# Dense experts of a graph network: logits and last bias on VectorE, tables made a stage earlier, one group finished ahead, inverse roots by Newton steps

## The reference, cut to what matters

```
feat = mean(x, axis=0)                      # one batch: feat = x
w = softmax(feat @ Wr + br)                 # 6250 x 8 shares
h = relu(bn(x @ W1[e] + b1, g1, be1, m1, v1))   # each expert e, 256 -> 256
h = relu(bn(h @ W2[e] + b2, g2, be2, m2, v2))
y = h @ Wo[e] + bo[e]
out = sum over e of w[:, e] * y[e]          # added to x
```

## Time and profile before

| | |
|---|---|
| median of 3 runs (lowest, highest) | 4462.22 us (4454.69, 4463.83) |
| profiled execution, its own time | 4459.09 us |
| its span, first to last instruction | 4457.3 us |
| mean granted TensorE clock over the span | 0.814 |
| TensorE matmul, weight load | 3334.8 us (75%), 2512.1 us (56%) |
| VectorE | 2672.3 us (60%) |
| ScalarE | 1572.2 us (35%) |
| GpSimd | 2067.7 us (46%) |
| dense stage, first to last instruction | about 3331 to 4457 us |
| second rows stage | about 1916 to 2091 us |

### The profile page before, as it was taken

One profiled execution on the slowest core, in us unless ns is written; L12 is line 12 of the kernel. 1 busy time (PEld: TensorE's weight loads), 2 busy tenths in 40 slices (PEclk: granted clock), 3 DMA queues, 4 the chain that ended last, 5 costly groups with the idle time before them and its releaser, 6 DMA issues. The chain is left out here.

```text
span 4457.3 us, 72937 instructions
## 1 busy us (share of the span) xinstructions
PE 3334.8 (75%) x16240; PEld 2512.1 (56%) x16240; DVE 2672.3 (60%) x8449; ACT 1572.2 (35%) x4383; POOL 2067.7 (46%) x2095
## 2 busy tenths in 40 slices
PE   5276667776666789964566666666659999999999
PEld 3144444444444578843344444444438888888888
DVE  8488999999987866654565565656555322222221
ACT  2233343334332224431333333333323434333343
POOL 0477777777770034365777777777730000000000
PEclk9677787777876579966677777777779999999999
DMA  4344444444454147644444444444461000000000
GB/s 123 81 106 107 107 108 107 107 107 107 107 99 87 37 126 193 171 114 99 107 106 106 106 106 106 105 106 105 105 80 35 5 7 5 7 5 7 5 7 8
DMA packets 386919, 369.85 MB, mean 83 GB/s; under 512 B 253644, under 2 KB 313708, under 8 KB 386562
## 3 DMA queue, kind: packets, MB, share of 16 engines
q0 software_dynamic: 107072, 272.84, 24.9%
q1 hardware_dynamic: 277094, 92.40, 9.4%
q10 hardware_dynamic: 2396, 0.84, 0.1%
HBM read 324.13 MB, written 41.59 MB: 82 GB/s over the span
## 5 line engine op out<-in xcount | busy, mean ns | idle before, releaser
L694 POOL DMA_INDIRECT g_G<-rows,g_pack x1856 | 1806.8, 973 | 756.1 <-issue 480.0
L727 PE MATMUL bank<-g_G,g_MB 128*125 128x260 f32 x1856 | 654.7, 499 | 207.1 <-DVE acc L933 205.9
L933 DVE SCALAR_TENSOR_TENSOR acc<-acc,g_c,bank 125x65 f32 (+1 forms) x2320 | 618.2, 315 | 147.5 <-PE bank L727 73.1
L1375 DVE SCALAR_TENSOR_TENSOR X<-bank,e_cw,X 125x256 f32 (+1 forms) x400 | 175.2, 479 | 795.6 <-PE bank L1201 795.6
L727 PE MATMUL bank<-g_G,g_M 128*125 128x257 f32 x1856 | 633.6, 489 | 20.7 <-DVE acc L933 20.6
L727 PEld LDWEIGHTS bank<-g_G,g_MB 128*125 128x125 f32 x1856 | 418.4, 243 | 348.9 <-DVE acc L933 242.4
L1271 ACT ACTIVATE e_h<-bank,e_bi_c,e_sc_c 128x250 f32<-128x250 f32 x800 | 403.6, 555 | 560.3 <-PE bank L1192 422.3
L798 ACT ACTIVATE g_mt_d<-bank,unode 125x256 bf16<-125x256 f32 x928 | 383.3, 463 | 457.7 <-PE bank L712 457.2
L727 PEld LDWEIGHTS bank<-g_G,g_M 128*125 128x125 f32 x1856 | 418.3, 241 | 147.4 <-DVE acc L933 26.5
L1201 PE MATMUL bank<-e_w,e_h 128*125 128x256 f32 x1600 | 379.3, 380 | 3.1 <-ACT e_h L1271 3.1
L1192 PE MATMUL bank<-e_h,e_w 128*128 128x250 f32 x1600 | 377.6, 378 | 1.2 <-ACT e_h L1271 1.2
(11 more groups left out here) (299 smaller groups left out, 4141.3 us busy)
## 6 DMA issues: line engine op xcount, KB each, us to landing
g_G<-rows,g_pack POOLq DMA_INDIRECT x1856
acc<-in_edge_attr SPq DMA_DIRECT2D x50, 476.0 KB
g_pack<-edge_pack SPq DMA_DIRECT2D x928, 2.0 KB
g_drow<-edge_dst SPq DMA_DIRECT2D x928, 1.0 KB
expert_out<-x_y SPq DMA_DIRECT2D x54, 256.0 KB
g_qe<-edge_q SPq DMA_DIRECT2D x464, 1.0 KB
rows<-acc SPq DMA_DIRECT2D x25, 227.5 KB
rows<-n_T SPq DMA_DIRECT2D x25, 224.9 KB
```

The costliest lines, as they stand in the source:

```text
L694: nc.gpsimd.indirect_dma_start(G[:, r, q, :], None, rows_d[l], bass.IndirectOffsetOnAxis(ap=pack[:, r, q, 0:1], axis=0)).then_inc(S(p + f" ...
L727: mm_ = nc.tensor.matmul(sum_bank(r, k, u)[0:TN, 0:HW], left, G[:, rk, q, :], start=(c == 0), stop=(c == C - 1))
L933: ins = nc.vector.scalar_tensor_tensor(at, at, c1[:, rk, u, h:h + 1], sum_bank(r, k, u)[0:TN, h * W:(h + 1) * W], ALU.mult, ALU.add)
L1375: ins = nc.vector.scalar_tensor_tensor(xt, bank[4 + u][0:TN, 0:D], cw[:, r, u, e:e + 1], xt, ALU.mult, ALU.add)
```

## The change

- Router: `rows(1)` turns the router matrix and stores it to DRAM (`router_d`); the dense stage loads it to all partitions (`wrb`, 1 MB). Each logit is a multiply with sum on VectorE (`dot`: 16 per group, four in each of the slots 1 to 4), `shares` moves to slot 5, `weigh` to slot 5, `normal_shares` to slot 6, `normal` to slot 1, `turn` to slot 4. `logits`, `turn_shares` and `turned_shares` go.
- Last bias: `bo` is loaded to all partitions (1 MB); `add_bias` runs on VectorE for each expert, in every slot, behind the collect of the expert before. `last_bias` on TensorE goes.
- Tables of the batch norm, and the weights of expert 0, are loaded in `rows(1)`, the tables turned and finished there. They lie in SBUF through `attention(1)`.
- One group is finished ahead, with a root on ScalarE; group 1 is finished in slot 1 of group 0, and groups 2 to 24 in slots 3 to 6 of groups 0 to 5. Their inverse roots come from a bit trick and three Newton steps on VectorE (`root`, 12 operations on up to 8 columns). The first 6 groups (`STATIC`) are written out instead of 4.

```diff
 # rows(1): loads on SyncE ahead of its loop
+ for q, nm in enumerate(names):
+     sp.dma_start(etab_r[q * NX:(q + 1) * NX, :], a[nm]).then_inc(S("etab_in"), 16)
+ sp.dma_start(ewr[:, :, :], a["L1_ffn_Wr"]...).then_inc(S("etab_in"), 16)
+ sp.dma_start(br[:, :], ...).then_inc(S("ebr_in"), 16)
+ for k, nm in enumerate(("L1_ffn_W1", "L1_ffn_W2", "L1_ffn_Wo")):
+     sp.dma_start(wa[k], a[nm][0, :, :]...).then_inc(S("ewa_in"), 16)
 ...
   run(sp, slot)
+ sp.wait_ge(S("ewrT"), 1)
+ sp.dma_start(router_d, ewrT[:, :]).then_inc(S("router_out"), 16)
+ sp.wait_ge(S("router_out"), 16)
 # rows(1), i == 3: TensorE turns the tables and the router, ScalarE copies them out and takes 2 roots;
 # VectorE behind its loop: 10 operations to scale and shift
 # dense_experts, SyncE
- for e in range(NX): ... 3 weights each
+ for c in CUTS:
+     sp.dma_start(wrb[c, :, :], router_d.unsqueeze(0).broadcast_to([TN, NX, D])[c])...
+ load(1)
+ for c in CUTS:
+     sp.dma_start(bo[c, :, :], a["L1_ffn_bo"].unsqueeze(0).broadcast_to([TN, NX, D])[c])...
+ for e in range(2, NX):
+     load(e)
 # ScalarE, slot
  relu(1, ...); relu(0, i, i * NX + e, e)
+ if isinstance(i, int) and i == 0 and e == 1:
+     weigh(0)
  if follows(i):
-     if e == 2: turned(i + 1, 1 - r)
-     if e == 4: weigh(i + 1)
-     if e == 5: turned_shares(i + 1)
+     if e == 4: turned(i + 1, 1 - r)
+     if e == 5: weigh(i + 1)
 # VectorE
+ def dot(g, r, e):
+     if e == 0:
+         v.wait_ge(S(p + "xn"), g + 1)
+         held(v, p + "xn_seen")
+     for u in range(GT):
+         n_ = e * GT + u
+         if n_ >= 2:
+             v.wait_ge(S(p + "dot"), g * NX * GT + (n_ - 1))
+         nc.vector.tensor_tensor_reduce(junk[:, n_ % 2, :], xn[:, u, :], wrb[:, e, :], 1.0, 0.0, ALU.mult, ALU.add,
+                                        dots[:, r, u, e:e + 1]).then_inc(S(p + "dot"), 1)
+ def add_bias(i, r, e):
+     if e:
+         v.wait_ge(S(p + "o"), i * NX + e)
+     else:
+         v.wait_ge(S(p + "xn"), i + 1)
+         v.wait_ge(S(p + "cw"), i + 1)
+     held(v, p + "o_seen")
+     for u in range(GT):
+         xt = xtile(i * GT + u)
+         ins = nc.vector.scalar_tensor_tensor(xt, bo[:, e, :], cw[:, r, u, e:e + 1], xt, ALU.mult, ALU.add)
+     ins.then_inc(S(p + "biased"), 1)
  def slot(i, r, t):
      for e in range(NX):
+         if follows(i) and e == 6: normal_shares(i + 1, 1 - r)
          collect(...)
+         add_bias(i, r, e)
          if follows(i):
+             if e == 1:
+                 if isinstance(i, int) and i == 0:
+                     finish(1)
+                     root(1, FIRST)
+                 normal(i + 1)
+             if 1 <= e <= 4:
+                 dot(i + 1, 1 - r, 2 * e - 2)
+                 dot(i + 1, 1 - r, 2 * e - 1)
+             if e == 5: shares(i + 1, 1 - r)
+             if early and e >= 3 and lo + e - 3 < hi:
+                 finish(lo + e - 3)
+     if early:
+         root(lo, hi)
+ invert(0, GT)
+ finish(0)
  ...
  normal(0)
+ invert(GT, NT)
+ v.wait_ge(S(p + "wrb_in"), ND)
+ for e in range(NX):
+     dot(0, 0, e)
  shares(0, 0)
  normal_shares(0, 0)
+ v.wait_ge(S(p + "bo_in"), ND)
```

More of the change, by code:

```diff
@@ L155, in xtile, with rows @@
             return X[:, bass.ds(t, 1), :].rearrange("p o d -> p (o d)")
-        def rows(l, acc, pos_i, share, sc):
+        def rows(l, acc, pos_i, share, pre, sc):
             H = HEADS[l]
@@ L364, in slot @@
                             mm.then_inc(S(p + "xT"), 1)
+                        if l == 1 and isinstance(i, int) and i == 3:
+                            pe.wait_ge(S("etab_in"), 16 * (NQ + 1))
+                            for k in range(2):
+                                nc.tensor.transpose(bank[2][:, k * P:k * P + NQ * NX], etab_r[:, k * P:(k + 1) * P], ident[0:NQ * NX, 0:NQ * NX])
+                            for k in range(2):
+                                mm = nc.tensor.transpose(bank[3][0:NX, k * P:(k + 1) * P], ewr[:, k, :], ident[:, :])
+                            mm.then_inc(S("etab_mm"), 1)
                     run(pe, slot)
@@ L1088, in dense_experts @@
             p = "e_"
[L1089 to L1099, removed]
+            FIRST, STATIC, EACH = 2, 6, 4
+            sc_c, bi_c, br, wa = pre
+            w1, w2, w3 = (sb(p + f"w{k}", [P, NX - 1, 2, D], F32, sc) for k in range(3))
+            bo = sb(p + "bo", [TN, NX, D], F32, sc)
+            wrb = sb(p + "wrb", [TN, NX, D], F32, sc)
+            junk = sb(p + "junk", [TN, 2, D], F32, sc)
+            dots = sb(p + "dots", [TN, 2, GT, NX], F32, sc)
             den = sb(p + "den", [TN, NT], F32, sc)
@@ L1142, in _ @@
                 def _(pe):
[L1143 to L1146, removed]
                     def turn(g, r):
@@ L1915, in build @@
             acc = sb("acc0", [TN, NT * HEADS[0] * (D // HEADS[0] + 1)], F32, s0)
-            for part in (lambda s2: rows(0, acc, None, None, s2), lambda s2: attention(0, acc, s2)):
+            for part in (lambda s2: rows(0, acc, None, None, None, s2), lambda s2: attention(0, acc, s2)):
                 with ExitStack() as s2:
@@ L1934, in build @@
                 with ExitStack() as s2:
-                    rows(1, acc, pos_i, share, s2)
+                    rows(1, acc, pos_i, share, pre, s2)
                 end_stage()
             acc1 = acc[:, 0:NT * (D + 1)]
-            for part in (lambda s2: attention(1, acc1, s2), lambda s2: dense_experts(acc1, s2)):
+            for part in (lambda s2: attention(1, acc1, s2), lambda s2: dense_experts(acc1, pre, s2)):
                 with ExitStack() as s2:
```

201 lines of the change are left out of this document (90 added, 111 removed).

## The result

The changed kernel takes 4415.02 us (median of 4; 4410.27 to 4416.63) against 4463.02 for the kernel before in the same session: ratio 0.9885, 95% interval [0.9864, 0.9906]. The forecast was 4431 in a range of 4402 to 4465, so the sign and the range held, and the gain, 48.0 us, is half as large again as the 31.6 forecast. One profiled execution of an experiment (four groups ahead) was a disturbed one at a mean clock of 0.716; its trace isn't compared.

The account below looks back on a forecast made before the run. TensorE was taken to bound the dense stage (busy 200 of 200 us). Start -9.5, groups 1 to 5 +5.9, border -3.5, groups 6 to 23 -25.2, rows stage +0.7 sum to -31.6: 4431 us, range 4402 to 4465.

Parts of the forecast that it names:

- rows stage and up to the first dense instruction: Second rows stage, paced by GpSimd's gathers: ends on the late store of the router rows, +0.7 us (0 to 1.9).
- layer 1: Start of the dense stage: one group instead of four finished before the root, so the first layer starts 16.9 us earlier.
- given back in group 0: Group 0: late first collect, overfull VectorE slot 1, late shares and lower clock, less removed TensorE work: +7.4 us.
- groups 1 to 5: Five written-out groups that also finish four groups each: VectorE late at the shares, TensorE waits; +5.9 us together.
- border: Between groups 2 and 3: ScalarE's wait for all variances and its table reload go, -3.5 us.
- eighteen groups: Groups 6 to 23: TensorE's removed 2.27 us less a new wait of 0.86, 1.4 gained each, -25.2 us.
- the steady wait: Looped groups: bias ahead of shares delays exponential and the relu queued behind it; TensorE loses 0.86 us (0.72 to 1.0).
- C: Rival, 15%: the exponential's lateness does not reach TensorE; steady groups gain the full 2.27 us, total 4409.
- An early group: ... +1.2: Each early static group: -2.27 us of TensorE work, +2.7 wait at the shares, +0.75 for the clock.
- A: Rival, 15%: summing halves the dot's rate, pitch 0.69 us; loop still fits, six early groups cost 2 us each, total 4444.
- B: Rival, 12%: VectorE becomes the bound in slots 1 to 4, from a dot pitch of 0.75 us; at 0.85, total 4523.
- D: Rival, 8%: the clock falls at each looped group's wait of 0.86 us, +27 us, total 4458, no change.

Follow-up runs that it names:

- four groups ahead: Against the changed kernel, four groups instead of one are finished ahead of the first root, none in slot 1 of group 0: 4412.79 us, ratio 0.9893.
- three dots: Against the changed kernel, every dot is done three times, the extra two into a tile that nobody reads: 4579.13 us, ratio 1.0267.
- two dots: Against the changed kernel, every dot is done twice, the second into a tile that nobody reads: 4443.66 us, ratio 0.9964.

## Why the prediction was right, and where its sizes were off

From the spans, term by term (us, forecast and measured): rows stage and up to the first dense instruction +0.7, +0.3; layer 1 -16.9, -17.0; given back in group 0 +7.4, +4.9; groups 1 to 5 +5.9, -2.7; border -3.5, -4.0; eighteen groups -25.2, -30.2. Sum -31.6, -48.7 (by unrounded terms). The misses don't cancel: 8.6 us of the 17.1 by which the sum is off lie in groups 1 to 5, 5.0 in the looped groups, 2.5 in group 0. The first term is not resolved: from the rows stage's first gather to the attention's first it is 182.1 us against 181.1 before, and 177.7 to 182.1 in the other runs with the same rows stage. It is not longer by more than 2, the sign of being wrong that the prediction named. The rows stage and the border had no run of their own.

*Right in mechanism and size:* what TensorE loses a group (2.27 forecast; 43.63 - 41.29 = 2.34 by the run with the later exponential), the start, and the border, whose 47.59 became an ordinary group.

*Right in mechanism, the steady wait too large:* 0.86 forecast, 0.66 measured, so groups of 41.95 instead of the 42.2 named (and of C's 41.4). The gap ahead of the bias, taken as 0.40, is 0.14 (collect to bias 1.02, of which 0.88 is collect's), so the exponential is 1.02 late and not 1.28. The result lies nearer to rival C's 4409 than to the forecast's 4431, but C is not what happens: the lateness does reach TensorE, and two runs got 18.7 and 23.3 us by removing it.

*The step that failed is "An early group: ... +1.2" in "First six groups".* Groups 1 to 5 gain 0.6 each instead (less 0.36 once, at the entry into the loop), and the wait above 2 us, named as a sign of being right, was 0.72 in group 0 and 1.47 to 1.82 in the others. VectorE's lateness at the shares was put at 2.0; 1.07 was measured (static less looped group). The slots 3 and 4 were put at 6.37 and take 5.85 and 5.86 (group 4's collects at 3537.39, 3543.24 and 3549.10). The dot accounts for it: its pitch is 0.345, below the forecast's lower bound of 0.40, and not 0.48, so four dots are 0.54 less; the smaller gap ahead of the bias and a gap of 0.17 ahead of the next collect make up for each other. And the half of 1.5 us of clock put on each such wait didn't come: after waits of 1.47 to 1.82 the layer took 1.99.

*Group 0:* the wait in slot 1 was 3.81 (5.1 forecast), slot 1 on VectorE 9.16 (3352.04 to 3361.20) instead of 10.1 by the same dots and smaller gaps. The wait at the shares was 0.72 (2.7 forecast). What is lost behind the wait, 1.77, came in slot 1 and not at the shares, where 1.5 had been put.

*Rivals.* A: no dot of 0.69; a pitch of 0.69, made on purpose, left the loop unchanged and cost most static groups 4.5 to 5.1 each (A's 2 us counted from a pitch of 0.48 and without the clock). B: shown at three dots, absent at one. D: the granted clock from 3600 to 3800 us, in the loop, is 1.00.

On the bias the rows answer the question left open: with both wide sources in SBUF (L1390) 481 ns, with one in PSUM (L1400) 479. The rule of the Trainium skill that a scalar-tensor-tensor operation with two 32-bit SBUF sources runs at half rate ("Vector Engine (DVE) Microarchitecture Reference", section "Points that are easy to get wrong") is not borne out by this trace. By it the bias would take at least the 0.69 of a 512-wide operation (an estimate from that page and that row).

## What to carry to other kernels

When an operation is put between a result and the engine that consumes it, ask what is queued behind the consumer: here 1.02 us on VectorE, an engine half idle, cost 0.66 us of TensorE a looped group and 1.03 a static one through ScalarE's queue, and moving the consumer one slot later, without taking any work away, gave nearly half of the change's own gain again. Work that the first product waits for was paid nearly one for one (7.9 us for three finishes), so do there only what the first group needs, and put the rest into the first stretch in which that engine waits. An average of 42 busy in 200 says that an engine has room; the slots in which extra work stacks up (slot 1 of group 0, slots 3 and 4 of the static groups) have to be summed one by one.

## What the runs showed that was not expected

The multiply with a sum is issued every 0.345 us while each lasts 0.42 and its accumulator read 0.08: summing out cost less than a scalar-tensor-tensor operation of the same width (0.40). How long a layer takes behind a wait, and so the clock that it is granted, doesn't follow from the wait's length alone: layer 3 took 1.99 after 1.47 to 1.82, 3.44 after 2.00, and 2.78 to 3.75 after 3.81 or 3.82 in the runs with that wait in group 0. With two dots it took 2.90 or 3.78 after 4.24. With three it took 1.96 after 2.11 and 1.96 to 3.65 after waits of 2.85 that look alike. In the looped groups with three dots, where the wait for the relu is 3.19 to 3.21, there is an order: from one group to the next the layer took 3.67, 3.55, 3.36, 3.15, 2.93, 2.71, 2.50 and 1.99, then 3.68, 3.53 and so on down to 1.99 again (granted clock in that trace 0.51 from 4090 to 4092 us, in a group with 3.68; 1.00 from 4044 to 4046, in one with 1.99). So it isn't chance, and neither the wait's length nor the work ahead of it decides, since both are the same in every looped group. What does decide stays open.
